# Two graph attention layers in one kernel: row scores turned on VectorE, a finer last group, other orders and a shorter preparation at the layer change

## The reference

```
layer 0 (4 heads of 32):  Wh = x @ W
  e[i,j,h] = leaky_relu(s_src[i,h] + s_dst[j,h], 0.2)   where adj[i,j], else -9e15
  h0 = elu(softmax_j(e) @ Wh)
x1 = layernorm(x + h0)
layer 1 (hyperbolic):     xt = arctanh(|x1|) * x1 / |x1|      (|x1| clipped to 1 - 1e-7)
  e[i,j] = leaky_relu(xt[i].a[:128] + xt[j].a[128:], 0.2)     where adj[i,j], else -9e15
  h1 = proj(expmap0(softmax_j(e) @ xt))
out = layernorm(x1 + h1)
```

## Time and profile before

| | |
|---|---|
| median of 3 runs | 948.96 us (948.72 to 950.5) |
| the profiled execution | 949.88 us, span 946.1 us |
| PE, DVE, ACT, POOL busy | 840.5 (89%), 789.7 (83%), 660.4 (70%), 19.1 (2%) us |
| weight loads (PEld) | 686.9 us (73%) |
| granted TensorE clock, mean | 0.952 |
| DMA packets | 151344, of which 138182 under 512 B |

### The profile page before, as it was taken

One profiled execution on the slowest core, in us unless ns is written; L12 is line 12 of the kernel. 1 busy time (PEld: TensorE's weight loads), 2 busy tenths in 40 slices (PEclk: granted clock), 3 DMA queues, 4 the chain that ended last, 5 costly groups with the idle time before them and its releaser, 6 DMA issues.

```text
span 946.1 us, 23426 instructions
## 1 busy us (share of the span) xinstructions
PE 840.5 (89%) x10348; PEld 686.9 (73%) x10348; DVE 789.7 (83%) x1433; ACT 660.4 (70%) x846; POOL 19.1 (2%) x39
## 2 busy tenths in 40 slices
PE   6089699999899987999699979779999999999993
PEld 6089689988899987999699876435555555555551
DVE  4699499999988999999689998789495977777876
ACT  2598698999769998799698894876454463647112
POOL 1000000000000000000000000000000000000000
PEclk9589799999899999999799989889999999999997
DMA  8999999996577002301000505240704040321000
GB/s 151 160 184 128 193 109 140 190 125 65 113 129 97 25 2 69 69 14 14 1 14 25 124 2 112 77 101 1 208 16 90 12 89 18 84 65 37 12 18 7
DMA packets 151344, 73.06 MB, mean 77 GB/s; under 512 B 138182, under 2 KB 142792, under 8 KB 150984
## 3 DMA queue, kind: packets, MB, share of 16 engines
q1 hardware_dynamic: 146484, 54.68, 26.1%
q0 software_dynamic: 4608, 16.78, 17.2%
q10 hardware_dynamic: 148, 0.07, 0.0%
HBM read 83.96 MB, written 21.12 MB: 111 GB/s over the span
## 4 chain that ended last, share of the span: by engine, by line
PE 49%; DVE 26%; ACT 10%; SPq 5%; DMA 5%; issue 4%; POOL 0%; DVEq 0%; ACTq 0%; POOLq 0%
PE bank L552 30%; PE bank L542 19%; ACT ring L595 7%; SPq L320 5%; DVE ring L792 5%; DVE ring L805 4%; DMA adj_small<-in_adj_dram 3%; ACT below L644 3%; DVE ring L812 2%; DVE evac L819 2%; DVE ring L809 2%; DVE evac L834 1%; DMA even_masks<-adj_small 1%; DMA feat<-in_x_dram 1%; DMA s_rows<-score_rows 1%
## 5 line engine op out<-in xcount | busy, mean ns | idle before, releaser
L542 PE MATMUL bank<-moving,ring 128*128 128x99 bf16 (+1 forms) x6144 | 476.2, 224 | 27.0 <-DVE ring L812 21.3
L595 ACT ACTIVATE ring<-s_rows,scores 128x1024 fp8e4<-128x1024 f32 (+1 forms) x464 | 411.6, 975 | 71.0 <-PE bank L542 52.2
L542 PEld LDWEIGHTS bank<-moving,ring 128*128 128x128 fp8e4 x6144 | 399.0, 99 | 34.7 <-issue 18.5
L552 PE MATMUL bank<-moving,above 128*128 128x387 bf16 x1024 | 338.7, 331 | 12.3 <-DVE evac L973 6.9
L552 PE MATMUL bank<-moving,below 128*128 128x387 bf16 x1024 | 340.1, 332 | 0.0
L542 PE MATMUL bank<-moving,even_masks 128*128 128x99 bf16 x1280 | 176.1, 212 | 36.7 <-DVE ring L805 31.9
L644 ACT ACTIVATE below<-s_rows,scores 128x512 int8<-128x512 f32 x256 | 159.5, 710 | 67.1 <-PE bank L552 67.1
L552 PEld LDWEIGHTS bank<-moving,above 128*128 128x128 fp8e4 x1024 | 101.4, 99 | 84.6 <-issue 8.6
L552 PEld LDWEIGHTS bank<-moving,below 128*128 128x128 fp8e4 x1024 | 100.7, 98 | 71.8 <-issue 2.6
L542 PEld LDWEIGHTS bank<-moving,even_masks 128*128 128x128 fp8e4 x1280 | 125.5, 98 | 37.5 <-issue 26.5
L792 DVE TENSOR_SCALAR ring<-s_rows,neg_d 128x1024 uint8<-128x1024 f32 (+1 forms) x176 | 98.3, 630 | 19.1 <-DMA s_rows<-score_rows 8.8
(11 more groups left out here) (164 smaller groups left out, 527.8 us busy)
## 6 DMA issues: line engine op xcount, KB each, us to landing
adj_small<-in_adj_dram POOLq DMA_DIRECT2D x32, 512.0 KB, 14.9
s_rows<-score_rows SPq DMA_DIRECT2D x12, 512.0 KB, 5.1
s_rows<-score_rows SPq DMA_DIRECT2D x16, 256.0 KB, 3.9
feat<-in_x_dram SPq DMA_DIRECT2D x4, 512.0 KB, 5.7
values_kept<-even_masks SPq DMA_DIRECT2D x1, 2048.0 KB, 22.0
again<-adj_small SPq DMA_DIRECT2D x1, 2048.0 KB, 9.5
again<-values_kept SPq DMA_DIRECT2D x1, 2048.0 KB, 8.2
out_dram<-attended SPq DMA_DIRECT2D x7, 256.0 KB, 2.1
```

What stands on the lines that cost most here:

```text
L542: last = pe.matmul(acc[:, at + lo:at + hi], mask, moving[:, h, j, lo:hi], start=first, stop=(j == T - 1), skip_group_check=True)
L552: last = pe.matmul(bank[2 * t + b][:, 0:PARTS * K1], of_tile(run[y][:, :], j, R, t * P, (t + 1) * P), moving1[:, PLACE1[j // GT], j % GT, ...
L595: last = act.activation(of_tile(below, k, rows, 0, rows), s_row(c, h), ACT.Sign, bias=scores[:, g * ju + k, h:h + 1], saturate=False)
```

## The change

- `keep_rows1`: VectorE turns the scores with one `dve.transpose` (32 x 32 blocks) into `turned1` in each of the three preparations, and SP stores them with four DMAs of 128-byte pieces per batch. The first two batches become one (0 to 20). GpSimd clears `scores1` at the start.
- `prepare` leaves out the series for small norms (L903 to L908 and three of the later steps) and joins two steps into one; the smallest norm is looked at in `sum_up`, and below 0.1 the general path is taken.
- `weigh` is cut into two pieces, after units 3 and 4 of a chunk in place of one after unit 2; `elu_exp`, `close_chunk`, the first `prepare_tiles` and the first two `split_group` follow one or two units later.
- `ACT_CODE`: in the last chunk four V units in place of five. `DIRECT_CODE`: three of chunk 0's first twelve units no longer direct.
- Run 0's last group of eight tiles becomes two of four (`GROUPS0`); the pieces of the layer change are interleaved anew on VectorE and ScalarE, with the signs of run 1's first twelve tiles among the last preparation; the last chunk's exponential goes to `flat_mixed`.
- The search leaves run 1's masks; its words are read again from DRAM later (`load_again`, now three loads, and `search_again` after closings 0, 2 and 3). GpSimd clears `wrong`.

```diff
-    ACT_CODE = "AAVAAVAAVAAVAVAA" + 3 * (8 * "AAAV") + "AAVAAVAAVAAVAVAA"
-    DIRECT_CODE = "DDDDDDDDDDDD----" + ...
+    ACT_CODE = "AAVAAVAAVAAVAVAA" + 3 * (8 * "AAAV") + "AAVAAVAAAVAAVAAA"
+    DIRECT_CODE = "DDD-DD-DD-DD----" + ...
+    GROUPS = [(g * GT, (g + 1) * GT) for g in range(NG)]
+    GROUPS0 = GROUPS[:-1] + [(T - GT, T - RT), (T - RT, T)]
...
-        ROWS1 = [(0, 4), (4, EARLY_TILES[1]), MIDDLE_TILES, LATE_TILES]
+        ROWS1 = [EARLY_TILES, MIDDLE_TILES, LATE_TILES]
...
-            with nc.allow_non_contiguous_dma(reason="scores of one tile lie across partitions"):
-                dst = score_rows1[1, lo * P:hi * P].rearrange("(t p) -> p t", p=P)
-                sp.dma_start(dst, scores1[:, lo:hi, 1]).then_inc(rows1_out[batch], 16)
+            sp.wait_ge(rows1_turned, batch + 1)
+            for b in range(P // 32):
+                dst = score_rows1[1:2, lo * P:hi * P].rearrange("o (t b p) -> (o t) b p", b=P // 32, p=32)[:, b, :]
+                sp.dma_start(dst, turned1[b * 32 + lo:b * 32 + hi, batch, :]).then_inc(rows1_out[batch], 16)
...
+                    dve.transpose(turned1[:, n - 1, :], scores1[:, :, 1]).then_inc(rows1_turned, 1)
...
                 step(e.reciprocal(scratch, norm))
-                step(e.tensor_tensor(square, norm, norm, ALU.mult))
-                step(e.tensor_scalar(near, square, 1.0 / 9, 1.0 / 7, ALU.mult, ALU.add))
-                for c in (5, 3, 1):
-                    step(e.tensor_tensor(near, near, square, ALU.mult))
-                    step(e.tensor_scalar(near, near, 1.0 / c, None, ALU.add))
-                step(e.tensor_scalar(square, norm, 0.1, None, ALU.is_lt))
...
-                step(e.tensor_tensor(own, own, scratch, ALU.mult))
-                step(e.tensor_scalar(own, own, 0.5, None, ALU.mult))
-                step(e.tensor_tensor(near, near, own, ALU.subtract))
-                step(e.tensor_tensor(near, near, square, ALU.mult))
-                step(e.tensor_tensor(own, own, near, ALU.add))
+                step(e.scalar_tensor_tensor(out=own, in0=own, scalar=0.5, in1=scratch, op0=ALU.mult, op1=ALU.mult))
...
-                if 1 <= c <= 3 and i == 5 or c == 4 and i == 4:
+                if 1 <= c <= 3 and i == 7 or c == 4 and i == 5:
                     elu_exp(act, c - 1)
...
             signs(act, 0, 2)
             round_group(act, 2, 1)
             elu_exp(act, NC - 1)
+            signs(act, 0, 3)
+            round_group(act, 3, 0)
+            signs(act, 1, 0)
+            round_group(act, 3, 1)
             act_roots(act, 3, *LATE_TILES)
+            signs(act, 1, 1, 0)
             act_logs(act, 3, *LATE_TILES)
             act_exps(act, 3, *LATE_TILES)
-            round_group(act, 3, 0)
-            signs(act, 0, 3)
-            round_group(act, 3, 1)
-            for g in range(NG):
+            signs(act, 0, 4)
+            round_group(act, 4, 0)
+            round_group(act, 4, 1)
+            signs(act, 1, 1, 1)
+            for g in (2, 3):
                 signs(act, 1, g)
...
                     take_head(dve, c - 1, H - 1)
-                    weigh(dve, c - 1)
+                if i in (3, 4) and c > 0:
+                    weigh(dve, c - 1, i - 3)
...
             take_head(dve, NC - 1, H - 1)
             weigh(dve, NC - 1)
-            step(dve.memset(wrong, 0))
-            split_masks(dve, 0, 2)
             split_group(dve, 2, 2)
+            split_group(dve, 3, 0)
             for piece in range(5):
                 close_chunk(dve, NC - 1, piece)
-            for piece in range(4):
-                prepare_tiles(dve, 3, LATE_TILES, piece)
-            split_group(dve, 3, 0)
+            prepare_tiles(dve, 3, LATE_TILES, 0)
+            split_masks(dve, 0, 2)
             split_group(dve, 3, 1)
+            prepare_tiles(dve, 3, LATE_TILES, 1)
             split_masks(dve, 0, 3)
             split_group(dve, 3, 2)
-            for g in range(NG):
+            prepare_tiles(dve, 3, LATE_TILES, 2)
+            prepare_tiles(dve, 3, LATE_TILES, 3)
+            split_group(dve, 4, 0)
+            split_masks(dve, 0, 4)
+            split_group(dve, 4, 1)
+            split_masks(dve, 1, 0)
+            split_group(dve, 4, 2)
+            for g in range(1, NG):
                 split_masks(dve, 1, g)
```

More of the change, by code:

```diff
@@ L83, in two_layer_gat @@
     NG = T // GT
-    PLACE1 = [3, 0, 1, 2]
+    GROUPS = [(g * GT, (g + 1) * GT) for g in range(NG)]
+    GROUPS0 = GROUPS[:-1] + [(T - GT, T - RT), (T - RT, T)]
+    PLACE1 = [(j + T - GT) % T for j in range(T)]
     EARLY_TILES, MIDDLE_TILES = (0, 20), (20, 28)
@@ L283, in moving1_part, with side1, run_groups, groups_before @@
         def moving1_part(g, b, q):
-            return moving1[:, PLACE1[g], :, (b * PARTS + q) * K1:(b * PARTS + q + 1) * K1]
+            lo, hi = GROUPS0[g]
+            return moving1[:, PLACE1[lo]:PLACE1[lo] + hi - lo, (b * PARTS + q) * K1:(b * PARTS + q + 1) * K1]
+        def side1(g, b):
+            lo, hi = GROUPS0[g]
+            return (part, work)[b][:, 0:(hi - lo) * K1].rearrange("p (t k) -> p t k", k=K1)
+        def run_groups(e):
+            return GROUPS0 if e == 0 else GROUPS
+        def groups_before(e):
+            return sum(len(run_groups(k)) for k in range(e))
+        def wait_signs(engine, e, groups):
+            engine.wait_ge(signs1_ready[e % 2], sum(len(run_groups(k)) for k in range(e % 2, e, 2)) + groups)
         def shrink_adj(pool, n):
@@ L557, in first_run @@
         def first_run(pe):
-            for g in range(NG):
+            for g, (lo, hi) in enumerate(GROUPS0):
                 pe.wait_ge(group_ready, g + 1)
@@ L571, in later_run @@
                 pe.wait_ge(pair_taken, (e - 1) * RT + t + 1)
-                for j in range(T):
-                    if t == 0 and j % GT == 0:
-                        pe.wait_ge(group_ready, e * NG + j // GT + 1)
-                    last = attend(pe, e, t, j)
+                for g, (lo, hi) in enumerate(GROUPS):
+                    if t == 0:
+                        pe.wait_ge(group_ready, groups_before(e) + g + 1)
+                    for j in range(lo, hi):
+                        last = attend(pe, e, t, j)
                 last.then_inc(tile_ready, 1)
@@ L627, in act_exps, with signs @@
             act.activation(factors1[:, 0, lo:hi, :], factors1[:, 0, lo:hi, :], ACT.Exp).then_inc(factors1_given, 1)
-        def signs(act, e, g):
+        def signs(act, e, g, half=None):
             y = e % 2
-            if g == 0:
+            lo, hi = run_groups(e)[g]
+            mid = (lo + hi) // 2
+            lo, end = (lo if half in (None, 0) else mid), (hi if half in (None, 1) else mid)
+            if lo == 0:
                 act.wait_ge(s_run_in[e % S_SLOTS], 16 * (e // S_SLOTS + 1))
@@ L638, in signs @@
                     act.wait_ge(tile_ready, RT * (e - 1))
-            for j in range(g * GT, (g + 1) * GT):
-                if e == 0 and j == EARLY_TILES[1]:
-                    act.wait_ge(scores1_ready, 2)
-                if e == 0 and j == MIDDLE_TILES[1]:
-                    act.wait_ge(scores1_ready, 3)
+            if e == 0 and lo <= EARLY_TILES[1] < end:
+                act.wait_ge(scores1_ready, 2)
+            if lo <= MIDDLE_TILES[1] < end:
+                act.wait_ge(scores1_ready, 3)
+            for j in range(lo, end):
                 last = act.activation(of_tile(below_run[y][:, :].bitcast(I8), j, R, 0, R), s_rows1[e], ACT.Sign,
                                       bias=scores1[:, j, 0:1])
-            last.then_inc(signs1_ready, 1)
+            if end == hi:
+                last.then_inc(signs1_ready[y], 1)
         def close_func(act, q, n):
```

179 lines of the change are left out of this document (103 added, 76 removed).

## The result

The changed kernel takes 923.66 us (median of 4 runs, 922.71 to 925.88), the kernel before 948.84 beside it (948.52 to 950.5): ratio 0.9735, 95% interval 0.9718 to 0.9752. The profiled execution took 924.26 us, with a span of 922.2 and so 2.06 us outside it (before: 949.88, 946.1, 3.78).

What follows compares the result with a forecast made beforehand. Before 629 us TensorE, VectorE and ScalarE, all near full, bound the kernel together; after it TensorE alone. Terms -9, -2.4, -4, -1, -1, 0, -3 sum to -20.4: forecast 929.0 us, about one in ten each below 918 and above 942.

Steps and rivals of the forecast that it cites:

- main case: The whole kernel gains about as the summed terms say: own range 924 to 934 us, chance 0.49.
- rival (c): Layer change and chunk holes go to their lower bounds, -33.3 us; half way there, 922 us; chance 0.15.
- Rival (b): Store's hole goes, holes at chunk starts only move, layer change gives nothing: -11.4, 937.6 us; chance 0.15.
- (d): In the layer change ScalarE and VectorE wait for each other in turn: +26, 955 us; chance 0.05.
- store: Fourth chunk: 128-byte pieces remove TensorE's issue hole behind the 4-byte store, -9 us, bounds 0 and -11.6.
- shorter preparation: Fourth chunk: fewer VectorE steps in the preparation, less the added turn, -2.4 us.
- third chunk: At its start unit 3's mask precedes the weighing and TensorE's 4.0 us hole goes: -4 us, bounds 0 and -6.3.
- start of the fourth: TensorE holes of 1.9, 0.9 and 1.4 us replace one of 5.3: -1 us, bounds +1 and -3.
- second chunk: The smaller hole at the second chunk's start: -1 us, bounds 0 and -2.
- chunk 0: Three more XORs on VectorE, hidden by its wait for a score row: 0, or 3.7 us if uncovered.
- fifth chunk and layer change: ScalarE, ending at 622.1, sets the layer change; TensorE's next run starts at 625.5, not 628.76: -3 us, bounds -8 and +6.
- the searches moved ... at nothing: Second layer: searches moved to two later closings lie in VectorE's idle fifth: 0, at most 4.6 us each.

Runs made afterwards that it cites:

- experiment 6: Changed kernel with the weighing undivided after unit 2 again, exponential and closing two units earlier as before: 929.85 us, ratio 0.9814.
- experiment 1: Kernel before with only the scores turned on VectorE and stored in 128-byte pieces: 938.54 us, ratio 0.9875.
- experiment 8: Changed kernel with the longer preparation (series for small norms) back in all three preparations: 926.18 us, ratio 0.9765.
- 9: Changed kernel with chunk 0's three units direct again: 922.37 us, ratio 0.9736.
- experiment 11: Changed kernel with the four takes ahead of the next run's later masks, and the third rereading load after run 5's masks: 911.85 us, ratio 0.96.
- experiment 2: Changed kernel with the 4-byte store of the row scores put back, VectorE's turns kept: 928.15 us, ratio 0.9763.
- experiment 3: Changed kernel with four stores of small pieces to a spare tensor added in the second layer: 934.93 us, one execution.
- experiment 4: Changed kernel with three stores to a spare tensor added in layer one (third, fourth and fifth chunk): 930.12 us, one execution.
- run 5: Not a follow-up run: a stretch of the second layer inside the kernel, whose masks SP loads late in the changed kernel.

## Why the prediction was right, and where it wasn't

The direction, the place and the range (918 to 942) were right. At 923.7 the time is 5.3 us under the forecast, just under the main case's own range (924 to 934) and near rival (c)'s 922, and (c) is in good part what happened: the holes of the chunks went to their walked bounds and the layer change gave 6.6 of its 8, 2.3 of it by the shorter preparation. Rival (b), the holes only move, falls with experiment 6, where they come back with their 6.2 and 3.4 us; (d), the mutual waiting, never began: ScalarE's waits in the layer change are 5.8 us.

| term | forecast | measured | by |
|---|---|---|---|
| store | -9 | about -9 in the span (rest of the fourth chunk -9.6, less 0.6 of preparation) | 1, trace |
| shorter preparation | -2.4 | -2.9 in the trace, -2.1 to -2.9 in time | 8 |
| third chunk | -4 (walked -6.3) | -6.1 | trace, 6 |
| start of the fourth | -1 | -3.4 | trace, 6 |
| second chunk | -1 | -1.5 | trace, 6 |
| chunk 0 | 0 | 0; +2.2 at the start is scatter | 9 |
| fifth chunk and layer change | -3 | -4.3 (-6.6 less 2.3 of preparation) | trace, 8 |
| later runs | 0 | +1.1 | trace, 11 |
| outside the span | 0 | -1.7 | trace, 1 |

- *The store.* Cause and size held: 9.5 to 10.4 us by experiment 1's trace, and 11.6 by its time, of which 1.8 lie outside the span. The mechanism held in part: the instruction packets are late or slow behind 4-byte stores, but they don't simply stand in line with the pieces. In the kernel before, the last 4-byte packet ends at 452.6 and TensorE's large hole only begins at 453.56. The undoing in experiment 2 gave less than half of the price, so here a price measured by adding a thing to one program was not the price of taking it out of another. The Trainium skill, "Runtime: NRT & Kernel Launch", section "Instruction fetch mechanics", has the fetch of instructions mostly hidden. In experiment 3 it was, with a packet of 5.64 us and no hole; experiments 1, 2 and 4 show "issue" holes in layer one that come and go with 4-byte stores, so there it is not.
- *Right in size, wrong in place: the shorter preparation.* I put its 2.4 us into the fourth chunk, where VectorE is the fuller engine. By experiment 8 it brings 0.6 there and 2.3 in the layer change, 2.9 in all.
- *Mis-sized: the third chunk.* My walk gave -6.3, and I took -4 "for new friction". The trace shows -6.1. VectorE's 9 idle us did let it through; the discount had no ground.
- *Mis-sized: the fourth chunk's start.* The walk said holes of 1.9, 0.9 and 1.4; they are 1.98, 0.62 and 1.25. But I set 4.2 us of small holes against 5.3 of one large hole and forgot that the large one has a second price. Granted clock around it, kernel before and kernel after:

```profile
374.00:378.00 4.00, 3.09 (x38) 3.09 (x39) 4.00 (x5) 2.98 (x3) 0.00 (x0) 0.59 0.02 4
```

```profile
374.00:378.00 4.00, 3.13 (x64) 2.98 (x64) 4.00 (x7) 4.00 (x5) 0.00 (x0) 1.00 0.02 4
```

  The same busy time carries 38 matmuls at a mean clock of 0.59 and 64 at 1.00. The hole of 5.3 us brought the next 3.2 us to the lower level (1.2 GHz), which by an estimate costs half of it, 1.6; with the 1.5 us by which the holes themselves are shorter that is 3.1 of the 3.4. I had used just this for the third chunk and not here. But a hole of 2 us isn't safe: in experiment 2 the same first hole (1.99 us before 368.23) is followed by 3.3 us at a granted clock of 0.50, and in the changed kernel those of 2.35 and 2.87 us (before 524.22 and 572.82) by about as much. So the price by the earlier trace rows, 2.8 us for a hole of 4.0, is that of one hole, and doesn't hold for "each of these": the 5.3 us hole was followed by less time at half clock than the one of 4.0.
- *Mis-sized: the layer change.* The walk had ScalarE busy 55 us and waiting 7.8 from its unit 15 to its last sign, 62.8 us; it was 61.3 with 55.14 busy and 5.8 of waits. And unit 15 ended 4.0 us later against the chunk's start, not 5.8. These are 3.3 us, the difference from -3.3 to -6.6. By experiment 8, 2.3 of it is the shorter preparation: its last batch counts where ScalarE waits for it. The shape held in detail: the takes did stand behind run 1's last masks, and TensorE was done with run 0 7.2 us early, where I said 7. I read that as slack that ends inside the stage; it was the next thing to win, and experiment 11 won it. One row I misread: of the 40 signs from 605.56 only 32 are run 1's, and end near 625.2; all 40 end at 630.15, after run 1's first matmul at 628.76. The 622.1 doesn't hang on it, since I had counted to 626.
- *Failed: "the searches moved ... at nothing".* I priced the four instructions of VectorE and not the DMA that goes with them. SP's queue is in order, and the reload now waits for a search ahead of run 5's load: a hole of 2.07 us that was not there. This is a wait added to a queue, and what was queued behind it had to be named.
- *Small slips.* The two stores at 445.51 took 1.99 us of SP's queue, so 1.0 each and not 0.5; the four turned ones took 2.31, about as much as I gave them. The turn took 0.21 us, not 0.35. The waits of ScalarE that I listed add up to 7.7 at most, not 7.8. And my chances for "faster" add up to 0.92, not 0.91.
- *Not seen: 1.7 us outside the span.* Every kernel with the turned tile has 1.8 to 2.1 us there, also experiment 2 with the 4-byte store, and the kernel before 3.4 to 3.9 in its runs. What makes it is open.

## What to carry to other kernels

Walk the in-order queues unit by unit with the trace's own durations, price every hole with its clock, and then believe the walk: here each discount that I took from it was an error, and where the walk itself was off (the layer change, by 3.3 us) the gain was larger still. Where a step is moved, follow its DMAs' waits through the issuing queue, because an in-order queue turns a harmless wait into one for all that stands behind it. When an engine is "7 us too early" for something, look at what it waits for at once: that wait and the queue's were worth about 12 us together, as much as any part of the change.

## What the runs showed of the hardware

A store of single floats to DRAM lands late: 2560 pieces of 4 bytes took 14.1 us (experiment 2) and 18.9 (experiment 3), 512 and 1024 of them still 10.4 to 11.8, 2560 of 128 bytes 3.8, and the two halves of 2560 of 512 bytes 5.2 each (experiment 4). The pieces themselves are soon off the DMA engines: in experiment 3 the last 4-byte packet ends 5.2 us after the issue, 13.7 before the landing. Behind such a store packets with instructions took 2.4 to 5.6 us in place of 0.9 to 2.2 (experiments 3 and 4), or started 4 to 5 us late (the kernel before and experiment 2). TensorE can then stand for want of instructions where a matmul starts every 0.055 to 0.06 us (0.6 to 7.3 us in all), and did not in experiment 3, where one starts every 0.168 us. The DMA share is 0.01 in the two large holes (and 442 to 449 of experiment 2), so a low share doesn't clear the DMAs of a wait; these waits ended 1 to 2.2 us before the landing. TensorE's clock fell to half after some holes of 2.0 us and not after others. Turning 128x32 floats on VectorE takes 0.21 us.
